# Experts' loop with early row buffers and paired outputs; last batch routed in halves among the shared blocks

## The chip, the cores and the metric

One of the eight cores of a Trainium2 chip runs the kernel. The metric is device time in microseconds (us). Engines: PE (matrix products), ACT, DVE and POOL (elementwise work), SP, which here only starts DMA transfers; POOL starts its own indirect transfers.

## The reference

Four sequences of 1024 tokens, 256 numbers a token. First a power attention with 8 heads, then a layer of 64 experts, each with a residual and a layer norm (bias and constants left out):

```python
a = where(causal, (q @ k.T * scale)**2 * exp(gate), 0)     # 8 heads, 2 query heads a key head
x = layernorm(x + ((a @ v) / (sum(a) + 1e-6)) @ Wc)
scores = softmax(x @ gate_w.T)                              # 64 experts
w, idx = top_k(scores, 6); w /= sum(w)
buf[e, pos] = x[token]                                      # at most 768 rows an expert
eo = silu(buf @ w_gate.T) * (buf @ w_up.T) @ w_down.T       # hidden width 176
y[token] += eo[e, pos] * w                                  # scatter-add
x = layernorm(x + y + shared_swiglu(x))                     # hidden width 352
```

## The kernel before

`schedule()` writes one list of tasks; every engine's program walks that list in order and issues its own part of each task, with semaphores between the engines. So the place of a task in the list sets its place in the queue of each engine that takes part in it. Every fp32 product runs as three passes over a high and a low part (`wf_hi`, `wf_lo`, `xe_hi`, `xe_lo`, ...).

**Attention.** 32 heads (4 batches of 8), each in 20 units (`UNITS`): a unit is 128 keys against a group of 256 queries. PE makes the scores (line 686) and the products with v (1035, 1038); ACT squares; POOL adds the squares up (`nacc`, 1903) and masks the decays (1893, 1894). When a group's units are done, PE's `norm` (1048) sums `nacc` over the keys and projects. The routing of batches 0 to 2 (the steps of `ROUTE`) runs in the background of the next batch's units. Its last steps, `send0` to `send3` on DVE (1683 to 1689), make the slot numbers `slot_u`, and POOL scatters each row to its six experts' lists: `slots<-rows,slot_u`, 48 indirect DMAs of 128 rows a batch (1944).

**Shared blocks.** After attention come 8 blocks of 512 tokens. A block is two half-blocks of `gate_up` (18 products, 686) and `hidden` (ACT and DVE), then `shared_down` (40 products, 696). DVE adds the normed rows `xr`, loaded from `x_dram`, and SP stores the sum to `y_part[0]`. The last batch's routing stands in this list as well, its steps between the blocks (`route_some`); PE makes its `x1t`, `logit` and `count` products (1080, 1095). No expert's rows can be loaded before all scatters have landed (`s_scatter` in `rows_in`).

**Experts.** For each of 64 experts SP loads up to 512 of its rows into one of five buffers `xr` (889), PE transposes them (`turn_x`, 1138) into one of the two spare PSUM banks, ACT and DVE split them into `xe_hi` and `xe_lo`, PE does `gate_up` (18 products of 512 columns, line 686) and `down` (four tiles of 128 rows, 5 products each, 696). ACT scales each tile into one of three buffers `y_e` (1359), and POOL adds it to the tokens' rows in `y_part[x % 2]` by an indirect DMA with addition (1954), whose row numbers it reads from a column of `xr`. `xr` of expert x is free for expert x+5 when the adds of x have landed (`rows_wait`, `c_add`). A list's unused rows point to dummy rows behind the tokens' and are added too. Rows beyond 512 go through 4 jobs at the end: DVE finds them (`jobs`, 1745 to 1757) at expert 2; POOL fetches their rows at experts 32 to 35 (1963).

**End.** `y_part[0] + y_part[1]` is loaded, normed and stored.

Of the kernel before, what the change touches and what calls it, by code (L numbers as in the profile page):

```python
# [63 lines left out]
WS, XS, YS, HS, XE, RS = 4, 5, 3, 4, 4, 4  # L64
# [14 lines left out]
for g_ in range(1, NG):  # L79
# [3 lines left out]
UNITS_ALL = [(n, g, s) for n in range(HEADS) for g, s in UNITS]  # L83


NA, NS, NJ = 7, 2, 4


ROUTE = ([f"stat{j}" for j in range(TILES // 2)] + ["std"] + [f"norm{j}" for j in range(TILES // 2)] + ["store"]
         + [f"{what}{k}" for k in range(NG) for what in ("x1t", "logit")] + ["softmax0", "softmax1", "max", "index"]  # L90
         + [f"{what}{q}" for q in range(4) for what in ("hot", "chosen")] + ["chosen_bf", "weight0", "weight1", "count", "slots"]
         + [f"{what}{q}" for q in range(4) for what in ("again", "send")])

SENDS = 24
# [18 lines left out]
def schedule():  # L113
# [20 lines left out]

    def qkv_tasks(n):
        def column(which, r, tc):
            put_off.append((on_spare("col", n, which, r, tc), ("col_lo", n, which, r, tc)))
# [12 lines left out]
        return tasks  # L150
# [6 lines left out]
    def route_step(b, name):  # L157
        if name[:3] in ("x1t", "log") or name == "count":
            on_spare("route", b, name)
            if name == "count":  # L160
                on_spare("route", b, "taken")
        else:
            do("route", b, name)
            if name[:4] == "send":
                q = int(name[4:])
                to_send.extend(("scatter", b, k) for k in range(q * SENDS // 4, (q + 1) * SENDS // 4))
# [13 lines left out]
    load_at = {4: 3, 11: NG, 13: NG + 1, 18: NG + 2}  # L180

# [48 lines left out]
    for u, (n, g, s) in enumerate(UNITS_ALL):  # L230
        at = u % NU
        catch_up()
        if at == 0:
            if n + 1 < HEADS:
                if (n + 1) % H == 0:
                    must += gate_tasks((n + 1) // H)
                must += qkv_tasks(n + 1)
                first = 2 if (n + 1) % H == 0 else 0
                must_at = [first + i * (NU - ahead - first) // len(must) for i in range(len(must))]
        if u + ahead < len(UNITS_ALL):  # L240
            if UNITS_ALL[u + ahead][0] != n:
# [4 lines left out]
        for what, when in (("em", em_at), ("decay_f", f_at), ("em_mask", mask_at)):  # L246
            if at in when:
                n1, g1 = n + when[at] // NG, when[at] % NG
                if n1 < HEADS and (n1, g1) != (0, 1):
                    do(what, n1, g1)  # L250
        if s == 2 * g - 1:
            do("decay", n, g)
        if s == 2 * g + 1:
            do("yt", n, g)
            late += [(u + 2, "norm", n, g, 0), (u + 2, "project", n, g, 0), (u + 3, "project", n, g, 1)]
        if at in load_at:
            n1, g1 = n + load_at[at] // NG, load_at[at] % NG
            if n1 < HEADS:
                do("decay_in", n1, g1)
        run_late(u)  # L260
        if must and at in must_at:
            must.pop(0)()
        elif background and u >= step_from:
            route_step(n // H - 1, background.pop(0))
            step_from = u + 2
# [28 lines left out]
        if to_send and at in send_at:  # L294
            do(*to_send.pop(0))
        if at == 5 and n % H == 0 and n:
            assert not background and not to_send
            background = list(ROUTE)
# [18 lines left out]
    assert not background  # L317


    background = list(ROUTE)  # L320

    def route_some(count):
        for _ in range(min(count, len(background))):
            route_step(B - 1, background.pop(0))
# [16 lines left out]
    def shared_up(m):  # L341
        for half in range(2):
            do("gate_up", 2 * m + half)
# [19 lines left out]
    route_some(len(background))  # L363
# [3 lines left out]
    def turn(x_id):  # L367
        do("pick", x_id)
        for pair in range(tiles_of(x_id) // 2):
            on_spare("turn_x", x_id, pair)  # L370

    def down(x_id):
        for j in range(tiles_of(x_id)):
            on_spare("down", x_id, j)

    for x_id in range(2):
        do("rows_in", x_id)
    do("raw_in", 2)
    turn(0)
    for x_id in range(E + KJ):  # L380
# [7 lines left out]
        if x_id + 3 < E + KJ:  # L388
            do("raw_in" if x_id + 3 < E else "over_raw", x_id + 3)
        if x_id + 1 < E + KJ:  # L390
            turn(x_id + 1)
        do("gate_up", k)
        do("hidden", k, 0)
# [9 lines left out]
    down(E + KJ - 1)  # L403
# [18 lines left out]
def build(nc, xT, x, wall, wvall, wg, gw, bc, wffn, table, out):  # L422
# [3 lines left out]
    y_part = [nc.dram_tensor(f"y_part{i}", [N + CAP, C], F32).ap() for i in range(2)]  # L426
    x1_dram = nc.dram_tensor("x1_dram", [N, C], F32).ap()
# [21 lines left out]
    masked_nth, nadd_of, unit_of = {}, {}, {}  # L449
    nadd = 0  # L450
    for u, (n, g, s) in enumerate(UNITS_ALL):
        unit_of[n, g, s] = u
        if s >= 2 * g:
            masked_nth[u] = len(masked_nth) + 1
        if s < 2 * g:
# [10 lines left out]
    down_of = {x_id: spare["down", x_id, tiles_of(x_id) - 1] for x_id in range(E + KJ)}  # L466
# [3 lines left out]

    def f_nth(n, g):
        return n * (NG - 1) + g

    def em_nth(n, k):
        return n * NG + k + 1

    with ExitStack() as ctx:
# [48 lines left out]
        row_w = [sb(ctx, f"row_w{i}", [P, MT]) for i in range(XS + KJ)]  # L526
# [8 lines left out]
        with ExitStack() as att:  # L535
# [37 lines left out]
            nacc = [sb(att, f"nacc{i}", [P, R, GROUP]) for i in range(NJ)]  # L573
# [29 lines left out]
        with ExitStack() as last:  # L603
# [30 lines left out]
        s_std, s_sqrt, s_x1, s_x1_out, s_x1t_hi, s_x1t_out = (signal(k) for k in (  # L634
            "s_std", "s_sqrt", "s_x1", "s_x1_out", "s_x1t_hi", "s_x1t_out"))
        s_shift, s_soft, s_token, s_weight = signal("s_shift"), signal("s_soft"), signal("s_token"), signal("s_weight")
        s_chosen, s_slot, s_scatter = signal("s_chosen"), signal("s_slot"), signal("s_scatter")
# [40 lines left out]
        def av_bank(j):  # L678
            return bank[2 + j % NJ]
# [32 lines left out]

        def row_w_of(x_id):
            return row_w[x_id % XS if x_id < E else XS + x_id - E]
# [8 lines left out]
        def rows_wait(once, x_id):  # L723

            prev = x_id - XS
            if prev >= 0:
                once.wait_ge(c_add[prev % 2], added(prev))
            else:
                last = max(m for m in range(M) if m % XS == x_id % XS)
                once.wait_ge(*out_of(("shared_down", last, 1)))  # L730
# [30 lines left out]
        def sp_program(e):  # L761
# [83 lines left out]
            def route(b, name):  # L845
                if name == "store":
                    once.wait_ge(s_x1, b + 1)
                    e.dma_start(x1_dram[b * T:(b + 1) * T, :].rearrange("(j p) c -> p j c", p=P),
                                rows[:, :, 0:C]).then_inc(s_x1_out, 16)
                elif name[:3] == "x1t":  # L850
                    k = int(name[3:])
                    ts = slice(b * T + k * GROUP, b * T + (k + 1) * GROUP)
                    once.wait_ge(s_x1t_hi, b * NG + k + 1)
                    e.dma_start(x1t_dram[0, :, :, ts], f32(x1t_hi[:, :, :])).then_inc(s_x1t_out, 16)
                    once.wait_ge(*out_of(("route", b, name)))
# [8 lines left out]
            def shared_in(m):  # L864
                i, r = m % XE, m % XS
                ms = slice(m * MAIN, (m + 1) * MAIN)
                b = m * MAIN // T
                attention_over(once)
                once.wait_ge(s_x1_out, 16 * (b + 1))
                once.wait_ge(s_x1t_out, 16 * 2 * NG * (b + 1))  # L870
# [4 lines left out]
                if m >= XS:  # L875
# [1302 lines left out]
```

## Time and profile before

| | us |
|---|---|
| median of 3 runs | 2573.97 (2572.37 to 2574.27) |
| profiled execution | 2557.7 |
| its span, first to last instruction | 2555.9 |
| attention, to the last projection | 1757.4 |
| shared blocks and routing, to the first expert's `gate_up` | 1757.4 to 1932.0 |
| experts 0 to 60 | 1932.0 to 2454.4 |
| experts 61 to 63, the jobs, the last adds | 2454.4 to 2513 |
| sums, norm and stores | 2513 to 2555.9 |
| busy: PE / DVE / ACT / POOL | 2312 / 1398 / 1249 / 1578 |

The stages follow one another, so each has to be read by itself. A wait is charged to the engine and line that waited, and `<-` names what ended it.

### The profile page before, as it was taken

How to read it: one execution, taken by the hardware profiler on the slowest of the kernel's cores; microseconds unless marked ns; L12 is line 12 of the kernel's file. 1: busy time of each engine (PE TensorE's matmuls, PEld its weight loads, DVE VectorE, ACT ScalarE, POOL GpSimd, SP SyncE). 2: the span in 40 equal slices, each digit the busy share in tenths (PEclk: the TensorE clock that was granted, in tenths of full speed). 3: DMA queues.
4: the chain of work that ended last, by engine and by line, in shares of the span. 5: the costliest groups of instructions: out<-in, count | busy, mean ns of one | idle time of the engine just before them, and what ended most of it. 6: DMA issues, size and time to landing. Idle time of an engine off the chain costs nothing.

```text
span 2555.9 us, 34620 instructions
## 1 busy us (share of the span) xinstructions
PE 2312.3 (90%) x11876; PEld 1793.6 (70%) x11880; DVE 1397.8 (55%) x2813; ACT 1248.9 (49%) x2302; POOL 1578.3 (62%) x1421
## 2 busy tenths in 40 slices
PE   5999999999999899999999999998797999989981
PEld 4777776776767677776667777666685887778871
DVE  2444444445564454557445455745666766656664
ACT  3444444444434344343444443434234777767764
POOL 2566555544578654457855445784074888788885
PEclk8999999999999999999999999999798999999996
DMA  3766741122123112111411211224355999889987
GB/s 125 302 238 261 279 157 63 54 63 64 40 64 119 54 52 87 40 40 69 138 31 53 88 40 38 71 76 146 119 188 163 216 212 202 193 197 213 210 165 230
DMA packets 162663, 329.68 MB, mean 129 GB/s; under 512 B 17552, under 2 KB 98192, under 8 KB 162480
## 3 DMA queue, kind: packets, MB, share of 16 engines
q1 hardware_dynamic: 114144, 262.01, 30.4%
q0 software_dynamic: 48192, 65.04, 14.0%
q8 instruction: 97, 1.59, 0.3%
q14 instruction: 86, 0.70, 0.1%
q10 hardware_dynamic: 144, 0.33, 0.0%
HBM read 172.21 MB, written 155.11 MB: 128 GB/s over the span
## 4 chain that ended last, share of the span: by engine, by line
PE 61%; POOL 10%; DMA 9%; DVE 8%; issue 7%; ACT 5%; POOLq 0%; SPq 0%; ACTq 0%; DVEq 0%
PE bank L686 37%; PE bank L1038 13%; POOL slots L1944 4%; DMA y_part<-y_e,xr 4%; PE bank L696 4%; POOL nacc L1903 3%; PE bank L1048 3%; DMA xr<-slots 3%; POOL y_part L1954 2%; PE bank L1138 2%; PE bank L1035 1%; DVE acc L1563 1%; DMA w_raw_f<-in_wffn,job_w 1%; ACT a L1288 1%; DVE ub L1526 1%
## 5 line engine op out<-in xcount | busy, mean ns | idle before, releaser
L1903 POOL TENSOR_TENSOR nacc<-nacc,a 128x512 f32<-128x512 f32 (+1 forms) x384 | 448.0, 1167 | 286.7 <-ACT a L1292 137.6
L1038 PE MATMUL bank<-a,v 128*128 128x512 f32 x1024 | 529.3, 598 | 0.0
L1954 POOL DMA_INDIRECT y_part<-y_e,xr x256 | 436.5, 1705 | 119.2 <-issue 74.5
L1288 ACT ACTIVATE a<-bank,c_s 128x512 f32<-128x512 f32 x384 | 263.7, 687 | 164.2 <-PE bank L686 148.5
L686 PE MATMUL bank<-q_hi,k_hi 128*128 128x512 f32 (+1 forms) x640 | 324.4, 507 | 12.1 <-DVE ub L1526 6.0
L1292 ACT ACTIVATE a<-ub 128x512 f32<-128x512 f32 (+1 forms) x256 | 133.9, 523 | 394.5 <-DVE ub L1526 382.9
L1903 POOL TENSOR_TENSOR nacc<-a,a 128x512 f32<-128x512 f32 (+1 forms) x128 | 148.9, 1163 | 252.1 <-ACT a L1288 194.6
L1944 POOL DMA_INDIRECT slots<-rows,slot_u x192 | 198.3, 1033 | 163.0 <-DVE slot_u L1689 110.9
L1563 DVE SCALAR_TENSOR_TENSOR acc<-bank,rec,acc 128x256 f32<-128x256 f32 x512 | 223.3, 477 | 98.5 <-PE bank L686 94.5
L686 PE MATMUL bank<-q_lo,k_hi 128*128 128x512 f32 (+1 forms) x640 | 240.0, 375 | 0.0
L686 PE MATMUL bank<-q_hi,k_lo 128*128 128x512 f32 (+1 forms) x640 | 238.3, 372 | 0.0
L686 PE MATMUL bank<-xt_hi,w_hi 128*128 128x512 f32 x384 | 189.8, 494 | 34.8 <-DVE acc L1563 31.0
L686 PE MATMUL bank<-xe_hi,wf_hi 128*128 128x512 f32 (+3 forms) x504 | 206.2, 409 | 10.2 <-DMA xe_lo<-x1t_dram 10.2
L686 PE MATMUL bank<-wc_hi,yt_hi 128*128 128x256 f32 x512 | 205.7, 402 | 4.9 <-DVE acc L1563 4.9
L1038 PEld LDWEIGHTS bank<-a,v 128*128 128x128 f32 x1024 | 186.3, 191 | 33.2
L686 PE MATMUL bank<-xe_lo,wf_hi 128*128 128x512 f32 (+3 forms) x504 | 198.6, 394 | 0.0
L686 PE MATMUL bank<-xe_hi,wf_lo 128*128 128x512 f32 (+3 forms) x504 | 198.1, 393 | 0.0
L1504 DVE TENSOR_TENSOR q_lo<-bank,q_hi 128x512 fp32r<-128x512 f32 x128 | 88.5, 691 | 184.7 <-ACT q_hi L1267 184.7
L1048 PEld LDWEIGHTS bank<-ones,nacc 128*128 128x128 f32 x1024 | 133.5, 193 | 75.2 <-issue 60.8
L1267 ACT ACTIVATE q_hi<-bank 128x512 fp32r<-128x512 f32 x128 | 76.2, 596 | 214.8 <-PE bank L686 214.6
L1542 DVE TENSOR_TENSOR yt_lo<-bank,yt_hi 128x512 fp32r<-128x512 f32 x128 | 88.5, 691 | 168.9 <-ACT yt_hi L1300 168.9
L686 PEld LDWEIGHTS bank<-q_hi,k_hi 128*128 128x128 f32 x640 | 122.6, 192 | 71.5 <-issue 35.9
(212 smaller groups left out, 5671.6 us busy)
## 6 DMA issues: line engine op xcount, KB each, us to landing
slots<-acc SPq DMA_DIRECT2D x65, 816.0 KB, 7.2
w_raw_f<-in_wffn SPq DMA_DIRECT2D x66, 624.0 KB, 6.7
xr<-slots SPq DMA_DIRECT2D x64, 544.0 KB, 4.6
decay_all<-decay_dram SPq DMA_DIRECT2D x128, 128.0 KB, 3.4
w_hi<-w_dram SPq DMA_DIRECT2D x24, 384.0 KB, 4.7
w_lo<-w_dram SPq DMA_DIRECT2D x24, 384.0 KB, 5.4
sum<-y_part SPq DMA_DIRECT2D x16, 512.0 KB, 10.7
wc_hi<-wc_dram SPq DMA_DIRECT2D x24, 256.0 KB, 3.9
```

The lines of the kernel that those rows point to most:

```text
L686: ins = e.matmul(dst, a, b, start=first and i == 0, stop=last and i == len(passes) - 1, skip_group_check=True)
L696: ins = e.matmul(dst, a, b, start=first and n_ == 0 and p_ == 0, stop=n_ == len(steps) - 1 and p_ == len(passes) - 1, skip_group_check=True)
L1038: e.matmul(dst, v[n % 3][:, s, :], a32[u % NA][:, :, :], start=first, stop=False, skip_group_check=True).then_inc(s_av)
L1048: ins = e.matmul(av_bank(j)[:, k:k + 1], nacc[j % NJ][:, r, tt * P:(tt + 1) * P], ones[:, 0:1], start=(k == 0), stop=True, skip_group_chec ...
L1288: e.activation(squares, score_bank(u)[:, 0:R * w].rearrange("p (r t) -> p r t", r=R), ACT.Square, scale=c_s[b % 2][:, g * (g - 1) + s, h:h ...
L1292: e.activation(squares, ub[masked_nth[u] % 2][:, :, 0:w], ACT.Square).then_inc(s_sq)
L1504: e.tensor_tensor(lo, bank[6 + m % 2][:, :], f32(hi), ALU.subtract).then_inc(s_out_of[m % 2])
L1542: e.tensor_tensor(yt_lo[j % 2][:, :, :], av_bank(j)[:, :].rearrange("p (r t) -> p r t", r=R), f32(yt_hi[j % 2][:, :, :]), ALU.subtract).th ...
L1563: ins = e.scalar_tensor_tensor(out=part, in0=bank[6 + m % 2][:, tt * C:(tt + 1) * C], scalar=rec[j % 2][:, tt * R + r:tt * R + r + 1], in1 ...
L1903: e.tensor_tensor(out_, a, b, op).then_inc(s_nadd)
L1944: e.indirect_dma_start(out=slots, out_offset=bass.IndirectOffsetOnAxis(ap=slot_u[:, j, k:k + 1], axis=0), in_=rows[:, j, :], in_offset=Non ...
L1954: e.indirect_dma_start(out=y_part[part], out_offset=bass.IndirectOffsetOnAxis(ap=x_rows[:, j, TOKEN_COL:TOKEN_COL + 1].bitcast(U32), axis= ...
```

## The change

The experts' loop, with the buffers it touches (XS counts `xr`, YS counts `y_e`):

```diff
-WS, XS, YS, HS, XE, RS = 4, 5, 3, 4, 4, 4
+WS, XS, YS, HS, XE, RS = 4, 4, 4, 4, 4, 4
+KEPT = 8
 # rows_wait: when the buffer of expert x_id is free
-                once.wait_ge(c_add[prev % 2], added(prev))
+                once.wait_ge(s_spare, spare["turn_x", prev, MT // 2 - 1] + 1)
+                once.wait_ge(c_pick, prev + 1)
 # pick, DVE: keeps the row numbers
+                elif x_id >= KEPT:
+                    once.wait_ge(c_add[x_id % 2], added(x_id - KEPT))
+                e.tensor_copy(row_token[kept_at(x_id)][:, 0:n], rows_of(x_id)[:, 0:n, TOKEN_COL].bitcast(U32))
 # add_rows, POOL: unused rows now point to row NOWHERE
-                    in_=y_e[y][:, j, :], in_offset=None, bounds_check=N + CAP - 1, oob_is_err=True,
+                    in_=y_e[y][:, j, :], in_offset=None, bounds_check=N - 1, oob_is_err=False,
 # down: one task, and one spare bank, for two tiles; ACT still evicts and POOL still adds tile by tile
-        for j in range(tiles_of(x_id)):
-            on_spare("down", x_id, j)
+        for pair in pairs:
+            if pair < tiles_of(x_id) // 2:
+                on_spare("down", x_id, pair)
 # schedule, one expert
-        if x_id + 1 < E + KJ:
-            turn(x_id + 1)
-        do("gate_up", k)
+        do("gate_up", k, 0)
         do("hidden", k, 0)
+        if x_id + 1 < E + KJ:
+            turn(x_id + 1)
         ...
+        do("gate_up", k, 1)
         do("hidden", k, 1)
         ...
+        do("gate_up", k, 2)
         do("hidden", k, 2)
         if x_id:
-            down(x_id - 1)
+            down(x_id - 1, (0,))
         do("hidden", k, 3)
+        if x_id:
+            down(x_id - 1, (1,))
```

So the spare banks are used four times an expert instead of six, and an expert's rows are turned between the first and the second third of the gate products of the expert before it.

The last batch's routing is cut into two halves of 512 tokens, parts 3 and 4, of 27 steps each. Part 3's steps go one to a unit among the last 21 units of attention; its last six, and all 24 of its scatters, stand behind `gate_up` of half-block 0. Part 4's steps stand between `gate_up` and `hidden` of half-blocks 1 to 11:

```diff
+PARTS = [(b_, 0, TILES) for b_ in range(B - 1)] + [(B - 1, t_, TILES // 2) for t_ in (0, TILES // 2)]
-    route_some(10)
+    paces = [len(background) - 27, 4, 2, 1, 2, 2, 2, 3, 3, 2, 4, 2]
     shared_up(0)
     for m in range(M):
         ...
-        route_some(7)
         for pair in range(MAIN // GROUP):
             on_spare("shared_down", m, pair)
+        if m == M - 1:
+            do("rows_in", 0)
+            do("rows_in", 1)
         do("shared_out", m)
-        route_some(6)
 # in the loop over attention's units
-        if to_send and at in send_at:
+        if to_send and (at in send_at or n >= LAST):
             do(*to_send.pop(0))
+        if u - u_last == first_half_routed_at:
+            background = route_steps(B - 1)
```

The units of the last two heads are interleaved (`LAST_UNITS`), so that all groups of the last batch's first half are finished early; the tables `last_at` and `cols_at` place their decays and columns. Batch 2's last scatters, formerly one pair to about every second unit, go one pair to a unit from head 30 on.

`shared_down` is evicted by a copy on ACT instead of the addition on DVE: the normed rows are stored straight into `y_part[1]`, which formerly was filled with zeros, and the 8 loads of normed rows go.

```diff
-                e.tensor_tensor(y_e[y][:, js, :], bank[6 + m % 2][:, :].rearrange("p (j c) -> p j c", c=C), xr[r][:, js, 0:C],
-                                ALU.add).then_inc(s_out_of[m % 2])
+                e.activation(y_e[y][:, js, :], bank[6 + m % 2][:, :].rearrange("p (j c) -> p j c", c=C), ACT.Copy).then_inc(s_out_of[m % 2])
```

On SP, around the first experts, before (`xr<-slots` are an expert's rows, `w_raw_f` its weights, `y_part<-y_e` a block's store; `c_add` counts landed adds):

```order
L882 DMA y_part<-y_e 128x4x256 [waits s_out_of1,s_out_of0] x4
L889 DMA xr<-slots 128x1088 [waits s_scatter]
L889 DMA xr<-slots 128x1088
L862 DMA w_raw_f<-in_wffn 128x1248 [waits c_wl]
L889 DMA xr<-slots 128x1088
L862 DMA w_raw_f<-in_wffn 128x1248 [waits c_wl]
L889 DMA xr<-slots 128x1088
L862 DMA w_raw_f<-in_wffn 128x1248 [waits c_wl]
L889 DMA xr<-slots 128x1088
L862 DMA w_raw_f<-in_wffn 128x1248 [waits c_wl]
L889 DMA xr<-slots 128x1088 [waits c_add0]
```

and after:

```order
L961 DMA y_part<-y_e 128x4x256 [waits s_out_of1,s_out_of0] x3
L968 DMA xr<-slots 128x1088 [waits s_scatter]
L968 DMA xr<-slots 128x1088
L961 DMA y_part<-y_e 128x4x256 [waits s_out_of1,s_out_of0]
L946 DMA w_raw_f<-in_wffn 128x1248 [waits c_wl]
L968 DMA xr<-slots 128x1088
L946 DMA w_raw_f<-in_wffn 128x1248 [waits c_wl]
L968 DMA xr<-slots 128x1088
L946 DMA w_raw_f<-in_wffn 128x1248 [waits c_wl]
L968 DMA xr<-slots 128x1088 [waits c_pick,s_spare]
```

The first two loads of rows have moved ahead of the last block's store, and from the fifth on a load waits for the turn (`s_spare`) and the pick of the expert four before it in place of the adds.

On POOL, in head 30 (`slots<-rows` are batch 2's scatters, `nacc` the sums of squares), before:

```order
L1944 DMA slots<-rows,slot_u 49920x272 x2
L1903 TENSOR_TENSOR nacc<-a_5,a_6 128x512
L1903 TENSOR_TENSOR nacc<-nacc,f_b 128x512
L1918 COPY nacc<-a_0 128x2x128
L1944 DMA slots<-rows,slot_u 49920x272 x2
L1903 TENSOR_TENSOR nacc<-a_0,a_1 128x2x128
L1944 DMA slots<-rows,slot_u 49920x272 x2
L1903 TENSOR_TENSOR nacc<-a_2,a_3 128x512
L1893 TENSOR_TENSOR decay_all<-decay_all,tab 128x128
L1894 TENSOR_TENSOR decay_all<-decay_all,tab 128x128
L1903 TENSOR_TENSOR nacc<-nacc,a_4 128x512
```

and after:

```order
L2029 DMA slots<-rows,slot_u 49920x272 x2
L1990 TENSOR_TENSOR nacc<-a_5,a_6 128x512
L1990 TENSOR_TENSOR nacc<-nacc,f_b 128x512
L2029 DMA slots<-rows,slot_u 49920x272 x2
L2004 COPY nacc<-a_0 128x2x128
L2029 DMA slots<-rows,slot_u 49920x272 x2
L1990 TENSOR_TENSOR nacc<-a_0,a_1 128x2x128
L2029 DMA slots<-rows,slot_u 49920x272 x2
L1990 TENSOR_TENSOR nacc<-nacc,a_2 128x512
L2029 DMA slots<-rows,slot_u 49920x272 x2
L1990 TENSOR_TENSOR nacc<-nacc,a_3 128x2x128
L2029 DMA slots<-rows,slot_u 49920x272 x2
```

A pair of scatters now stands behind every unit's work, where two or three adds stood between pairs.

## Rows read from the trace of the kernel before

**Rows 1.** The page's part 4, by engine: shares of the chain that ended last

```profile
PE 61%; POOL 10%; DMA 9%; DVE 8%; issue 7%; ACT 5%; POOLq 0%; SPq 0%; ACTq 0%; DVEq 0%
```

**Rows 2.** Windows: busy us (count) of PE, PEld, DVE, ACT, POOL; clock; DMA; GB/s

```profile
1757.40:1767.90 10.50, 0.28 (x4) 0.08 (x2) 5.07 (x9) 3.77 (x3) 2.02 (x5) 0.67 0.76 262
1767.90:1932.00 164.10, 126.65 (x703) 109.55 (x705) 100.65 (x203) 47.65 (x78) 52.94 (x48) 0.85 0.51 176
1932.00:2454.40 522.40, 487.93 (x2788) 408.93 (x2787) 354.15 (x558) 387.49 (x668) 415.85 (x245) 0.98 0.89 201
2454.40:2513.00 58.60, 41.94 (x273) 37.14 (x271) 29.76 (x54) 32.04 (x66) 49.07 (x32) 0.93 0.72 117
2513.00:2556.00 43.00, 0.00 (x0) 0.00 (x0) 20.99 (x88) 19.30 (x41) 18.86 (x9) 0.50 0.77 298
```

**Rows 3.** Groups by shape, POOL, 1660:1757.4: busy us, mean ns | idle before

```profile
L1944 POOL DMA_INDIRECT slots<-rows,slot_u x30 | 29.6, 987 | 7.3 <-issue 5.6 <-POOL nacc L1903 1.6
L1903 POOL TENSOR_TENSOR nacc<-nacc,a 128x512 f32<-128x512 f32 x20 | 25.7, 1283 | 1.6
```

**Rows 4.** Timeline, attention's end: start, length [idle before <- releaser]

```profile
1664.96 0.99 POOL L1944 DMA_INDIRECT slots<-rows,slot_u  x1 [0.15 <-POOL nacc L1903]
1707.62 0.59 PE L1035 MATMUL bank<-a,v 128*128 128x256 f32 x2
1714.96 1.84 PE L1048 MATMUL bank<-ones,nacc 128*128 128x1 f32 x8 [4.07 <-POOL nacc L1903]
```

**Rows 5.** Waits, 1767 to 1932 us: us in total, times, longest

```profile
POOL slots L1944 <- DVE slot_u L1689: 94.5, 1, 94.5
POOL slots L1944 <- issue: 14.3, 47, 0.3
PE bank L1095 <- DVE chosen_bf L1644: 14.0, 1, 14.0
PE bank L1138 <- DMA xr<-slots: 13.7, 1, 13.7
```

**Rows 6.** Chain of waits, 1840 to 1960 us: start, us, what

```profile
1924.24 3.52 DMA xr<-slots
1927.81 1.13 PE bank L1138 x4
```

**Rows 7.** Chain of waits, experts, 2050 to 2120 us

```profile
2055.97 6.83 DMA y_part<-y_e,xr
2062.82 5.54 DMA xr<-slots
2069.50 4.15 PE bank L686 x18
2073.65 2.62 PE bank L696 x20
2076.33 1.16 PE bank L1138 x8
```

**Rows 8.** Waits, experts, 1932 to 2454.4 us

```profile
PE bank L1138 <- DMA xr<-slots: 25.2, 27, 4.2
PE bank L696 <- DVE xe_lo L1778: 6.2, 1, 6.2
```

**Rows 9.** Groups by line, POOL, 1932 to 2454.4 us

```profile
L1954 POOL DMA_INDIRECT y_part<-y_e,xr x237 | 404.4, 1706 | 113.4 <-issue 68.7 <-ACT y_e L1359 41.6 <-DMA y_part<-y_e,xr 3.0
L1963 POOL DMA_INDIRECT acc<-slots,job_rows x8 | 11.6, 1454 | 2.4 <-issue 2.1 <-DMA y_part<-y_e,xr 0.3
```

**Rows 10.** Timeline, POOL and DVE, 2263 to 2290 us

```profile
2268.30 1.55 POOL L1954 DMA_INDIRECT y_part<-y_e,xr  x1 [0.30 <-issue]
2268.77 1.45 DVE L1694 TENSOR_TENSOR wf_lo<-w_raw_f,wf_hi 128x1248 fp32r<-128x1248 f32 x1
2277.61 2.04 POOL L1954 DMA_INDIRECT y_part<-y_e,xr  x1 [0.30 <-issue]
2278.87 0.68 DVE L1708 TENSOR_TENSOR ha_lo<-h_a,ha_hi 128x512 fp32r<-128x512 f32 x1
```

More of the change, by code:

```diff
@@ L82, with before, diagonal, route_steps @@
 NU = len(UNITS)
[L83 to L94, printed above, removed]
+def before(n, g):
+    return [(n, g, s) for s in range(2 * g)]
+def diagonal(n, g):
+    return [(n, g, 2 * g), (n, g, 2 * g + 1)]
+LAST = HEADS - 2
+LAST_UNITS = (before(LAST, 1) + diagonal(LAST, 0) + diagonal(LAST, 1) + diagonal(LAST + 1, 0) + before(LAST + 1, 1)
+              + before(LAST, 2) + diagonal(LAST + 1, 1) + before(LAST, 3) + diagonal(LAST, 2) + diagonal(LAST, 3)
+              + before(LAST + 1, 2) + before(LAST + 1, 3) + diagonal(LAST + 1, 2) + diagonal(LAST + 1, 3))
+UNITS_ALL = [(n, g, s) for n in range(LAST) for g, s in UNITS] + LAST_UNITS
+GROUPS = [(n, g) for n, g, s in UNITS_ALL if s == 2 * g + 1]
+GROUP_NTH = {group: i for i, group in enumerate(GROUPS)}
+NA, NS = 7, 2
+PARTS = [(b_, 0, TILES) for b_ in range(B - 1)] + [(B - 1, t_, TILES // 2) for t_ in (0, TILES // 2)]
+def route_steps(p):
+    pairs = range(PARTS[p][2] // 2)
+    steps = ([f"stat{j}" for j in pairs] + ["std"] + [f"norm{j}" for j in pairs] + ["store"]
+             + [f"{what}{k}" for k in pairs for what in ("x1t", "logit")] + ["softmax0", "softmax1", "max", "index"]
+             + [f"{what}{q}" for q in pairs for what in ("hot", "chosen")] + ["chosen_bf", "weight0", "weight1", "count", "slots"]
+             + [f"{what}{q}" for q in pairs for what in ("again", "send")])
+    return [(p, step) for step in steps]
+SENDS = 6
 def f32(ap):
@@ L229, in schedule @@
         do("score", u)
-    for u, (n, g, s) in enumerate(UNITS_ALL):
-        at = u % NU
+    for u, (n_, g, s) in enumerate(UNITS_ALL):
+        n, at = divmod(u, NU)
         catch_up()
[L233 to L239, printed above, removed]
+        if at == 0 and n < LAST:
+            if (n + 1) % H == 0:
+                must += gate_tasks((n + 1) // H)
+            must += qkv_tasks(n + 1)
+            first = 2 if (n + 1) % H == 0 else 0
+            must_at = [first + i * (NU - ahead - first) // len(must) for i in range(len(must))]
         if u + ahead < len(UNITS_ALL):
-            if UNITS_ALL[u + ahead][0] != n:
+            if (u + ahead) // NU != n:
                 while must:
@@ L342, in shared_up @@
         for half in range(2):
-            do("gate_up", 2 * m + half)
+            for i in range(3):
+                do("gate_up", 2 * m + half, i)
+            route_some(paces[2 * m + half])
             hidden(2 * m + half)
-    route_some(10)
+    paces = [len(background) - 27, 4, 2, 1, 2, 2, 2, 3, 3, 2, 4, 2]
+    assert sum(paces) == len(background)
+    paces += [0] * (2 * M - len(paces))
     shared_up(0)
@@ L362, in schedule, with down @@
             do("split_lo", m - 2)
-    route_some(len(background))
+    assert not background and not to_send
     do("counted",)
     def turn(x_id):
-        do("pick", x_id)
         for pair in range(tiles_of(x_id) // 2):
             on_spare("turn_x", x_id, pair)
-    def down(x_id):
-        for j in range(tiles_of(x_id)):
-            on_spare("down", x_id, j)
-    for x_id in range(2):
-        do("rows_in", x_id)
+        do("pick", x_id)
+    def down(x_id, pairs):
+        for pair in pairs:
+            if pair < tiles_of(x_id) // 2:
+                on_spare("down", x_id, pair)
     do("raw_in", 2)
@@ L465, in build @@
             raw_loads += 1
-    down_of = {x_id: spare["down", x_id, tiles_of(x_id) - 1] for x_id in range(E + KJ)}
+    down_of = {x_id: spare["down", x_id, tiles_of(x_id) // 2 - 1] for x_id in range(E + KJ)}
     shared_down_of = {m: spare["shared_down", m, 1] for m in range(M)}
@@ L886, in rows_in @@
                 r = x_id % XS
[L887 removed]
+                all_sent(once)
                 rows_wait(once, x_id)
@@ new lines, in route @@
+                    once.wait_ge(s_chosen, p + 1)
+                    e.matmul(head, strict_bf[:, :], chosen_bf[:, tiles_in(p), :], start=True, stop=False, skip_group_check=True)
+                    for j in range(nt - 1):
+                        ins = e.matmul(head[:, j + 1:nt, :], ones_bf[:, :],
+                                       chosen_bf[:, t0 + j:t0 + j + 1, :].to_broadcast([P, nt - 1 - j, E]), start=False,
+                                       stop=(j == nt - 2), skip_group_check=True)
+                else:
+                    for j in range(nt):
+                        ins = e.matmul(ps[:, 0:E], ones_bf[:, :], chosen_bf[:, t0 + j, :], start=(j == 0), stop=(j == nt - 1))
@@ L1110, in gate_up @@
-            def gate_up(k):
+                product(e, bank[3 * (k % 2) + part][0:cols.stop - cols.start, 0:width], [
+                    (g_hi[:, c, cols], g_lo[:, c, cols], x_hi[:, c, :], x_lo[:, c, :]) for c in range(CC)]).then_inc(c_gu)
+            def gate_up(k, part):
                 w, i = job_of(k)
@@ L1171, in over_body @@
                 e.wait_ge(c_h, 2 * (k - 1))
-                gate_up_passes(k, w, xe_hi[0][:, :, 0:OVER], xe_lo[0][:, :, 0:OVER], OVER)
+                for part in range(3):
+                    gate_up_part(k, part, w, xe_hi[0][:, :, 0:OVER], xe_lo[0][:, :, 0:OVER], OVER)
                 e.wait_ge(c_hl, 2 * k + 2)
@@ L1581, in route @@
                     steps_done()
-                    for j in range(TILES):
+                    for j in each:
                         ins = e.bn_aggr(mv[:, j, :], stats[:, j, :])
@@ L1630, in route @@
                     steps_done()
-                    for j in range(TILES):
+                    for j in each:
                         ins = e.max_index(out=top8_at[:, j, :], in_max=top8[:, j, :], in_values=scores[:, j, :])
```

452 lines of the change are left out of this document (238 added, 214 removed).

## The prediction

> **What bounds the kernel now.** I read the page's chain first, then the windows by stage, then the waits and the chain inside each stage. The chain [rows 1] is PE for 61%, with POOL and DMA for about a tenth each; an average, so the windows [rows 2] come next. There the reader should see four different limits. In the shared blocks and routing (1767.9 to 1932.0) PE works 126.65 of 164.1 us. Its long waits are two [rows 5]: 14.0 us for `chosen_bf`, and 13.7 us for the first expert's rows, at the end of a chain: DVE makes `slot_u`, POOL scatters 48 times, the last scatter lands at 1924.24, the load takes 3.52 us, PE turns at 1927.81 [rows 6]. In the experts (1932.0 to 2454.4) PE works 487.93 of 522.4 us. The chain there [rows 7] is either PE's own period, 4.15 + 2.62 + 1.16 = 7.93, with gaps about 7.98, or a detour: landing of adds 6.83 us, then the load of rows 5.54 us, which waited for them, then PE. PE lost 25.2 us to such loads and 6.2 us once behind `jobs` on DVE [rows 8]. From 2454.4 to 2513 POOL's adds set the end, 49.07 us busy of 58.6. The last 43 us, which the change leaves alone, stay as they are.
>
> **Experts' loop.** The wait on adds leaves SP's queue; on that queue stand the weight loads, which were held up behind it. Rows of x+4 now wait for the turn and pick of x, four periods earlier than they are needed, against a load of 5.54 us [rows 7]. So the 25.2 us go. What is late next? The candidates are POOL and the two spare banks. POOL: 237 adds, mean 1.706 us [rows 9], start to start 0.30 more, as between two scatters, 14.3 us in 47 gaps [rows 5]: 2.006, four an expert 8.02. This is PE's 7.98 to within the reading. At their best the adds take 1.55 [rows 10], 7.4 an expert, so POOL can catch up half a us a period. Skipping unused rows is not in the trace; of four adds of 1.56 it saves between nothing and, at a quarter of the rows unused, 1.56 us. I take nothing, since no row shows that an add's length follows its rows. DMA moves less by it: its share of 0.89 [rows 2] need not rise with the pace.
>
> Eight fetches for the jobs at experts 32 to 35 cost POOL 8 × (1.454 + 0.30) = 14 us [rows 9]. Before, this lag passed through `c_add` to PE at once. Now four `y_e` buffers let POOL lag about two periods, 16 us, so PE does not feel it; the lag melts at up to half a us a period over 28 experts, 14 us, and the rest (0 to 12, I take 3) is paid after expert 61. The paired banks leave four uses an expert, each about 1.16 to 1.3 of PE, then ACT, then DVE for a turn: my sum round them is 7.0 to 7.2 us, an estimate just below the period. ACT's 387 and DVE's 354 of 522 us [rows 2] leave room for the small copy of row numbers, so it costs nothing; without that cover, some 0.2 us a period, 12 in all. So experts 0 to 61: 60 × 7.98 + 5.4 (the first, without `down`: 7.98 − 2.62) + 6.2 (`jobs`, bounds 0 to 8.7) = 490.4 against 522.4: −32.0. With the lag of 3: **−29** (range −10 to −36).
>
> A rule speaks against this. Two adds of 1.55 and 2.04 lie in [rows 10]: the first beside DVE's `wf_lo`, the second beside `ha_lo`, both with two inputs in SBUF. The Trainium skill, "GPSIMD Engine Reference", its opening table, says that POOL shares its SBUF interfaces with VectorE and contends with DVE instructions that have two SBUF inputs. By that rule all of `wf_lo`, `ha_lo` and `hb` would be added to a nearly always busy POOL. The trace agrees for `ha_lo` at most, and not for `wf_lo`: 1.55 beside it. The mean of 1.706 holds what is so stretched now.
>
> **Shared blocks.** Before: 10.5 + 164.1 = 174.6 us from the end of attention to expert 0. After, POOL has 24 scatters behind the last `send` instead of 48. A scatter costs 52.94/48 + 0.30 = 1.40 [rows 2, 5], so 33.6 us. The sends stand behind half-blocks 10 and 11, so PE has then done eleven half-blocks of gate products, 11 × 4.15, four blocks of downs, 4 × 2 × 2.62, at a granted clock below full at first, 4 us more, and 4 us of routing products: 74.6. DVE, which has the routing of a half-block in front of `hidden`, comes 12 to 15 us later: 88.5. Then 33.6, landing 1.5, load 3.5, turn and split 4.2 (1927.81 to 1932.0): 131.3. PE's own sum is shorter: 8 × (2 × 4.15 + 2 × 2.62) = 108, with the same 8 and some waits 116 to 123. The first half's 24 scatters are hidden, as POOL had nothing there (its wait was 94.5 us long [rows 5]). DVE's eviction goes to ACT, busy 47.65 of 164.1 [rows 2]. The loads of normed rows and the zero fills lie on queues with room, at nothing. So 10.5 + 131.3 = 141.8, **−32.8** (range −40, PE alone, to −25, DVE 8 us later).
>
> **Attention's end.** Here the change costs. POOL's rows are nearly gapless there, 30 scatters at 0.987 us and adds of 512 at 1.283 [rows 3]. PE already waited 4.07 us for `nacc` at 1714.96 [rows 4]. In the new order a pair of scatters (0.99 + 0.30 + 0.98 and some idle, 2.35) stands behind every unit of head 30. From POOL's place at 1664.96 [rows 4] to the mask of head 31, group 1, stand 14 pairs, 32.9 us, and about 21 us of adds and masks: POOL is there at 1718.5. PE's norm for that group comes just behind the av that ran at 1707.62 [rows 4], and waits. What is left for PE behind that norm: 42.7 us from 1714.96 to 1757.7 as before, 3.3 that formerly ran ahead of its wait, 1.4 net for half the routing's short products against one group's norm and projections that are done sooner (an estimate, 0 to 5): 47.4. End 1765.9 instead of 1757.4: **+8.5** (range 0, POOL shorter, to +20, a second such wait).
>
> **Sum.** −29 − 32.8 + 8.5 = −53.3; I round the shared stage's and attention's unknown waits up by 2: −51. The profiled execution took 2557.7 us, span 2555.9 and 1.8 around it; it would become 2506.7. The median of the runs, 2574.0, stands 16.3 above that execution, and I move it by the same amount: 2523.
>
> **Rivals.**
> 1. POOL paces the loop. For: 8.02 against 7.98, and the fetches. Against: at 1.55 it would be faster than PE. Time: POOL's 277 instructions of both windows take 415.85 + 49.07 us [rows 2] and 277 × 0.30 between them, 548, against 568 from expert 0's first add, 13 us behind 1932 (4.15, `hidden` and 2.62), to 2513: −20; 6 to 7 of that is lost again behind `jobs`: −13 instead of −29. With the others 2537.
> 2. The chain round the two spare banks is longer than the period. A turn for x+1 now lies inside `gate_up` of x, so `xe_hi`, `xe_lo`, `pick`, `h_a`, `split_lo`, `hb` and `y_e` follow on ACT and DVE in one row, and a down can't start before the turn's bank is evicted. For: ACT and DVE are 74% and 68% busy, in strict order. Against: my sum of 7.0 to 7.2. The other stages give −24, so from a period of 8.86 the change is slower than before (522.4 + 24 = 546.4, less 11.6 and the lag of 3, over 60). At 9.2 it is 2574 + 20 = 2594.
> 3. Attention's end is later by 23 instead of 8.5, if PE stands a second time behind POOL, masks and scatters in a row: 2537. For: POOL's rows; against: after the 14 pairs only adds are left.
> 4. By the rule of two SBUF inputs, each period of POOL is 7.4 + 1.45 + 0.68 + 0.69 = 10.2 instead of 7.98, 64 times: some 2665. The adds of 1.55 beside `wf_lo` speak against it.
>
> **How the numbers follow.** Forecast 0.62; rival 1: 0.20; rival 3: 0.11; rival 2: 0.05; rival 4: 0.02. The forecast's own terms reach from −76 to −15, the ends seldom all together, so 2500 to 2545 holds most of it; rivals 1 and 3 lie inside. Range 2498 to 2552. The measurement tells 0.2%, about 5 us, from no change: faster 0.92, same 0.03, slower 0.05 (rivals 2 and 4, less the mild ends of 2, and a little for what I did not see).
>
> **What would show it.** Attention's last product near 1766, with PE waiting some 8 us for `nacc` before the norm of head 31, group 1. PE's first turn about 127 us after the first `gate_up`, and the last scatter just before it; 24 scatters between the blocks. In the experts no wait of PE for `xr`, periods of 7.98 except around `jobs`, the same through experts 32 to 40; POOL's wait for `y_e` small. It is wrong if PE waits for ACT or DVE in most periods, if periods stay near 8.5, or if the first turn still stands behind `xr` by more than 10 us.

## The result

The changed kernel takes 2553.99 us (median of 5 runs, 2550.01 to 2560.44) against 2573.97 (2566.74 to 2578.99): ratio 0.993 (0.9915 to 0.9944), some 20 us less where 51 were forecast, and just outside the range given. Side by side on another occasion the two took 2540.46 and 2557.58, ratio 0.9931 (0.9907 to 0.9955). The runs below were made on three chips, and the kernel before differs from one to the next: 2557.6 us on chip 3, 2573.4 on chip 13, 2554.9 on chip 9 (for the first result the chip is not on record). So each run is set against the kernel before on its own chip.

The windows of the changed kernel, by the same stages as [rows 2] (busy us and count of PE, PEld, DVE, ACT, POOL; granted clock; DMA share; GB/s):

```profile
1771.60:1781.40 9.80, 0.00 (x0) 0.00 (x0) 4.08 (x6) 3.77 (x3) 1.92 (x4) 0.67 0.75 266
1781.40:1926.40 145.00, 122.08 (x664) 102.52 (x664) 79.52 (x160) 54.86 (x92) 52.35 (x49) 0.93 0.45 151
1926.40:2440.00 513.60, 479.90 (x2861) 412.92 (x2862) 358.78 (x641) 364.13 (x681) 416.21 (x240) 0.98 0.83 192
2440.00:2507.00 67.00, 32.93 (x206) 29.73 (x204) 21.10 (x43) 23.08 (x51) 55.92 (x37) 0.76 0.50 79
2507.00:2549.00 42.00, 0.00 (x0) 0.00 (x0) 19.86 (x88) 19.30 (x41) 19.64 (x10) 0.50 0.78 303
```

Attention ends at 1771.6 (1757.4 before). The shared blocks and routing take 145 us (164.1 before). The loop and its tail take as long as they did: 513.6 + 67.0 against 522.4 + 58.6.

The chain of the changed kernel by engine, against [rows 1]:

```profile
PE 53%; POOL 16%; issue 12%; DVE 9%; ACT 5%; DMA 4%; POOLq 0%; another core or an unknown queue 0%; SPq 0%; ACTq 0%; DVEq 0%
```

DMA's share has fallen from 9% to 4%, as it should when no load of rows waits for adds, and POOL's has risen from 10% to 16%. POOL's groups in the loop, against [rows 9], show why:

```profile
L2039 POOL DMA_INDIRECT y_part<-y_e,row_token x232 | 407.0, 1754 | 109.9 <-issue 67.7 <-ACT y_e L1450 38.9 <-DMA y_part<-y_e,row_token 3.3
L2047 POOL DMA_INDIRECT acc<-slots,job_rows x8 | 9.6, 1205 | 2.4 <-issue 2.4
```

The add has not become shorter but longer: 1.754 us in place of 1.706. And PE, which no longer waits for `xr`, waits for ACT's `y_e`, which waits for adds to land before it may overwrite an output buffer (1926 to 2440 us):

```profile
ACT y_e L1450 <- DMA y_part<-y_e,row_token: 52.8, 20, 5.7
PE bank L1216 <- ACT y_e L1450: 27.2, 24, 3.9
```

[rows 8] had 25.2 us of PE on rows. The wait changed its name and kept its size, because behind both stood POOL's adds. POOL had hardly been idle before, either. From the first add to the last, its 264 adds took 448.9 us, the 0.30 us in front of each instruction 81.3 and the fetches 11.6, which leaves 25.8 of 567.6; in the changed kernel 458.4, 81.3 and 9.6 leave 18.2 of 567.6. Waits taken off PE could shorten the loop by no more than this idle time, as long as the adds did not get shorter.

**Where an add gets long.** The timeline of POOL and DVE in two periods of the changed kernel, some 120 us into the loop:

```profile
2041.78 1.54 POOL L2039 DMA_INDIRECT y_part<-y_e,row_token  x1 [0.30 <-issue]
2042.03 1.45 DVE L1785 TENSOR_TENSOR wf_lo<-w_raw_f,wf_hi 128x1248 fp32r<-128x1248 f32 x1
2043.51 0.69 DVE L1797 TENSOR_TENSOR h_b<-bank,silu_b 48x512 f32<-48x512 f32 x1
2043.63 2.60 POOL L2039 DMA_INDIRECT y_part<-y_e,row_token  x1 [0.30 <-issue]
2044.12 0.68 DVE L1799 TENSOR_TENSOR ha_lo<-h_a,ha_hi 128x512 fp32r<-128x512 f32 x1
...
2049.49 1.45 DVE L1785 TENSOR_TENSOR wf_lo<-w_raw_f,wf_hi 128x1248 fp32r<-128x1248 f32 x1
2050.24 2.11 POOL L2039 DMA_INDIRECT y_part<-y_e,row_token  x1 [0.30 <-issue]
2052.38 0.69 DVE L1802 TENSOR_TENSOR hb<-h_b,hb 48x512 fp32r<-48x512 f32 x1
2052.66 1.83 POOL L2039 DMA_INDIRECT y_part<-y_e,row_token  x1 [0.30 <-issue]
```

What counts is what DVE does at the moment an add *starts*. At 2041.78 no such operation runs yet; `wf_lo` begins 0.25 later, lies beside the rest of the add, and the add takes its 1.54. At 2050.24 `wf_lo` is running and ends 0.70 later: the add takes 0.57 longer. At 2052.66 `hb` ends 0.41 later: 0.28 longer. At 2043.63 `h_b` runs with `ha_lo` right behind it; `ha_lo` ends 1.17 after the add's start: 1.05 longer. The add loses the time to the end of the operation, less some 0.12 (of `ha_lo`'s end where that follows at once). Counted over 256 adds of each trace (the first eight left out), by DVE's operation at the start; "lost" is the sum of the lengths over 1.55:

| DVE at the add's start | SBUF operands | before: adds, lost us | after: adds, lost us |
|---|---|---|---|
| `wf_lo` | two | 53, 33.1 | 36, 19.1 |
| `hb` | two | 55, 4.2 | 28, 7.1 |
| `ha_lo` | two | 7, 0.4 | 3, 0.1 |
| `h_b`, `ha_lo` behind it | one, then two | 0 | 23, 22.9 |
| `h_a` | one | 10, 0.1 | 26, 0.0 |
| `xe_lo` | one | 16, 0.1 | 56, 0.0 |
| nothing or a short one | | 115, 0.8 | 84, 0.0 |

Back to back, POOL's period is 4 × 1.85 and what it loses, and its starts walk through PE's period of 7.43 until they meet every one of these operations. PE's own period, which the prediction had left at 7.98, had fallen to 7.43, and it bought nothing.

### The profile page after: what moved, and what is told of

Its sections match the earlier page's. It is cut to its first block, busy times and chain, and to the rows that moved or that the text cites. A ratio compares the mean times of both kernels' runs of the same rounds, so it can differ in the third digit from the quotient of the medians.

```text
span 2549.3 us, 34748 instructions
## 1 busy us (share of the span) xinstructions
PE 2296.0 (90%) x11880; PEld 1786.2 (70%) x11880; DVE 1383.8 (54%) x2884; ACT 1227.5 (48%) x2323; POOL 1585.3 (62%) x1422
## 4 chain that ended last, share of the span: by engine, by line
PE 53%; POOL 16%; issue 12%; DVE 9%; ACT 5%; DMA 4%; POOLq 0%; another core or an unknown queue 0%; SPq 0%; ACTq 0%; DVEq 0%
PE bank L769 33%; PE bank L1117 12%; POOL y_part L2039 8%; POOL nacc L1990 4%; PE bank L1127 3%; POOL slots L2029 3%; DMA y_part<-y_e,row_token 2%; PE bank L779 2%; PE bank L1114 1%; DVE acc L1653 1%; ACT a L1370 1%; DVE ub L1618 1%; DVE yt_lo L1632 1%; ACT yt_hi L1381 1%; ACT a L1374 0%
## 5 line engine op out<-in xcount | busy, mean ns | idle before, releaser
L2039 POOL DMA_INDIRECT y_part<-y_e,row_token x264 | 458.4, 1736 | 119.8 <-issue 77.5
L2029 POOL DMA_INDIRECT slots<-rows,slot_u x192 | 197.6, 1029 | 138.3 <-DVE slot_u L1780 86.7
```

The source lines that it names most:

```text
L2029: e.indirect_dma_start(out=slots, out_offset=bass.IndirectOffsetOnAxis(ap=slot_u[:, j, k:k + 1], axis=0), in_=rows[:, j, :], in_offset=Non ...
L2039: e.indirect_dma_start(out=y_part[part], out_offset=bass.IndirectOffsetOnAxis(ap=token, axis=0), in_=y_e[y][:, j, :], in_offset=None, boun ...
```

## The experiments

The changed kernel's second execution and the three runs behind it are from chip 3, the two with the routing moved, the dummy rows and the undivided `gate_up` from chip 13, the last four from chip 9.

**The changed kernel again**, as a partner for the next three.

> The changed kernel once more, as the partner for the next runs. Both theories: 2554, within 6; POOL again adds back to back from expert 3 to the end, with a mean near 1.74 us an add.

2540.46 (0.9931), mean add 1.736; less than the 2554 expected, as the kernel before is faster on this chip too. This execution is the better one to hold against [rows 2], as its routing stage lacks the stalls that the first has (last section): attention to 1773.5, then 142.9 us to expert 0, loop from first to last add 565.4 us, against 1757.7, 174.3 and 567.6 before.

**`h_a` and `h_b` in PSUM.** The product is written back into its own bank, so `ha_lo` and `hb` have one operand in SBUF; PE's wait before it overwrites the bank moves from `c_h` to `c_hl`.

```diff
-e.tensor_tensor(h_a[:, 0:width], bank[b0 + 1][:, 0:width], silu_a[:, 0:width], ALU.mult).then_inc(c_h)
+e.tensor_tensor(bank[b0 + 1][:, 0:width], bank[b0 + 1][:, 0:width], silu_a[:, 0:width], ALU.mult).then_inc(c_h)
-e.tensor_tensor(ha_lo[i][:, 0:width], h_a[:, 0:width], f32(ha_hi[i][:, 0:width]), ALU.subtract).then_inc(c_hl)
+e.tensor_tensor(ha_lo[i][:, 0:width], bank[b0 + 1][:, 0:width], f32(ha_hi[i][:, 0:width]), ALU.subtract).then_inc(c_hl)
 # h_b, hb, ACT's reads of h_a and h_b likewise
-                once.wait_ge(c_h, 2 * (k - 1))
+                once.wait_ge(c_hl, 2 * (k - 1))
```

> h_a and h_b are written back into their PSUM banks instead of SBUF, so the DVE operations ha_lo and hb read one operand from SBUF instead of two; nothing else changes. Theory 1 (an add of POOL that starts while a DVE operation with two SBUF operands runs, or is about to run, waits until that operation ends; in the trace after, the adds that start in wf_lo lose 19 us, in hb 7 us, in h_b with ha_lo behind it 23 us, all others nothing): the 30 us of hb and ha_lo go, the starts shift and wf_lo takes some 5 more; mean add 1.64, time 2554 - 25 = 2529 (2522 to 2539). Theory 2 (the long adds wait for room in the DMA queue): mean add and time unchanged within 5 us. Theory 3 (PE's period, 7.43, sets the loop and POOL only follows): unchanged.

2504.98, ratio 0.9795 (0.9772 to 0.9819); 35.5 us less than the changed kernel on the same chip, and 2502.18, 0.98, on chip 9. POOL's adds over the whole run, from the changed kernel's again and from this one:

```profile
L2039 POOL DMA_INDIRECT y_part<-y_e,row_token x264 | 458.4, 1736 | 111.1 <-issue 73.1
```

```profile
L2037 POOL DMA_INDIRECT y_part<-y_e,row_token x264 | 415.9, 1575 | 117.6 <-issue 80.9
```

DVE's work is the same, some operations even 0.01 to 0.02 us longer; 42.5 us of POOL's time are gone. `ha_lo`, `hb` and `h_b` now cost the adds 0.1 us in all, and `wf_lo` 5.6 instead of 19. My reading, which no run tested by itself: a POOL that runs at PE's pace keeps its place in the period and meets `wf_lo` less. I had expected the opposite there, hence 35 us instead of 25. Theories 2 and 3 fall.

**And `wf_lo` shortened** to 16 columns from expert 4 on; the low parts of the other weights are left out.

```diff
+                cols = slice(0, 16) if 4 <= x_id < E else slice(None)
-                e.tensor_tensor(wf_lo[w][:, :], w_raw_f[r % RS][:, :], f32(wf_hi[w][:, :]), ALU.subtract).then_inc(c_wl)
+                e.tensor_tensor(wf_lo[w][:, cols], w_raw_f[r % RS][:, cols], f32(wf_hi[w][:, cols]), ALU.subtract).then_inc(c_wl)
```

> As the run before, and from expert 4 on wf_lo is computed for 16 of its 1248 columns only (the low parts of the other weights are those of an earlier expert, so the output is not the reference's). Theory 1: no add is longer than 1.6 but for the four of expert 60 and later, 7.4 us of POOL an expert against 7.43 of PE; time 2554 - 45 = 2509 (2503 to 2517). Theory 2: as the changed kernel, 2554.

2497.08 (0.9769, 0.9743 to 0.9796): mean add 1.556, lost 1.6 us in all, the floor. 8 us less than the run before; in the traces 5.4 of it is the loop (519.3 us), and 4.4 is an attention that ended earlier, which the edit does not touch. The estimate of 45 in sum was 43.

**The kernel before with `h_a` and `h_b` in PSUM.**

> The kernel before with h_a and h_b in PSUM. Theory 1: there 33 of the 39 us that its adds lose are lost in wf_lo and only 5 in hb and ha_lo, so 2574 - 3 (2564 to 2576). Theory 2: unchanged. If it gains 20 us or more, the gain of the second run is not from the adds.

2547.66 (0.9968, 0.9953 to 0.9983), 10 us less, where 3 were expected: the adds take 3.3 us less in all (mean 1.69), as expected, and the rest is not explained here. `wf_lo` still costs 34.5 us. With it the table is closed; us from the first add to the last:

| | `h_a`, `h_b` in SBUF | in PSUM |
|---|---|---|
| loop before | 567.6 | 560.2 |
| loop changed | 565.4 | 524.7 |

The change of the loop is worth 2 us with `h_a` and `h_b` in SBUF and 35.5 with them in PSUM; executions of one kernel differ by 1 to 2 us here. Of the 35.5, 29.7 are shorter adds (445.6 us in all against 415.9), since `wf_lo` costs 34.5 us in one kernel and 5.6 in the other. The kernel before without `wf_lo`'s share was not run, so what the change is worth with no contention at all is not shown.

**The last batch's first half routed after attention**, and then also the scatters at their old places.

```diff
         if u - u_last == first_half_routed_at:
             assert not background
-            background = route_steps(B - 1)
-    background += route_steps(B)
+    background = route_steps(B - 1) + route_steps(B)
 # the second of the two, besides
-        if to_send and (at in send_at or n >= LAST):
+        if to_send and at in send_at:
```

> The changed kernel with all 27 steps of part 3's routing behind gate_up of half-block 0; the units' order and the scatters of batch 2 as in the changed kernel. Of the 14 to 16 us by which attention ends later, theory 1 puts about 5 on DVE, whose routing steps stand in front of acc, nrm and ub in the last 21 units, and 6 on PE's wait for nacc behind POOL's scatters. Then attention ends near +10 instead of +15, and the shared stage grows by 10 to 15 us (21 steps of DVE in front of hidden 0): +5 to +10 against the changed kernel. Rival: the interleaved heads alone cost it; then attention's end stays at +15, and the whole is +12 or more.

> As the run before, and batch 2's scatters at every second unit, as in the kernel before; what is left of them goes behind gate_up of half-block 0. Theory 1: the wait of 5.6 us for nacc in head 30 goes, attention ends at +4 or less against before. Rival: attention's end unchanged against the run before, so POOL's scatters were not its cause.

2565.03 (0.9964) and 2563.10 (0.9958). The changed kernel's 0.9931 is from chip 3, and on chip 13, where these ran, it was not measured, so these ratios do not say that they are slower. What can be set beside them are the next two runs, from the same chip and with the routing as changed (`h_a` and `h_b` in PSUM): attention ends there at 1773.4 and 1773.7 and expert 0 starts at 1949.1 and 1950.3. Here attention ends at 1763.6 and 1760.4 and expert 0 starts at 1941.1 and 1933.9, 8 us earlier and more.

So the routing steps cost attention 10 us. They lie behind the norm of head 31, group 1: from its start to attention's end it is 53.4 to 54.0 us in all nine executions with the steps in attention, and 44.8 without them. They are not DVE's alone, at which I had put 5: from 1555 us to attention's end PE is busy 5.0 us less than in the run with dummy rows (192.6 against 197.6; the steps' 32 products are 3.7 of it) and idle 4.8 less. In the second run the wait for `nacc` did not go, as expected, but moved to the next group's norm and grew. PE's waits in attention's last 100 us there:

```profile
PE bank L1126 <- POOL nacc L1989: 8.0, 1, 8.0
PE bank L1116 <- DVE nrm L1637: 0.6, 1, 0.6
```

Its 3 us are no more than two executions of one kernel differ by (1757.7 and 1760.0 before), so what POOL's scatters cost attention and what the units' order costs it is not told apart.

Behind attention the steps save little on this chip: the way to expert 0 is 177.5 and 173.4 us, against 175.7 and 176.7 with the routing as changed. On the other two chips, where that way takes 143 to 147 us, this was not tried.

**Unused rows added to dummy rows again** (with PSUM): `base=N`, `bounds_check=N + CAP - 1`, `y_part` of `N + CAP` rows.

> The changed kernel with h_a and h_b in PSUM, and unused rows added to dummy rows again instead of skipped. Theory: an add's length on POOL does not follow the rows that it moves (1.55 us undisturbed in both kernels), so the time is that of the same kernel with skipping, 0.9795 of before, within 4 us; DMA's share in the loop rises by some 0.05. Rival: DMA, at 0.89 before, is next in line and sets the pace: 10 us or more longer.

2534.11 (0.9851, 0.9823 to 0.9879), 13 us over the expected time by the ratio of the kernel with skipping; but not in the loop, which takes 522.9 us (524.7 with skipping) at a mean add of 1.579. The longer part is the routing stage, 176 us instead of 145, with the stalls of the last section; all four runs from this chip have them. DMA's share from 1940 to 2450 is 0.96 instead of 0.83, and nothing waits for it. Skipping saves transfers, not time.

**The turn in front of an undivided `gate_up`** (with PSUM; the pairs stay).

```diff
-        do("gate_up", k, 0)
-        do("hidden", k, 0)
         if x_id + 1 < E + KJ:
             turn(x_id + 1)
+        for i in range(3):
+            do("gate_up", k, i)
+        do("hidden", k, 0)
         ...
-        do("gate_up", k, 1)
         ...
-        do("gate_up", k, 2)
```

> The changed kernel with h_a and h_b in PSUM, and the turn of the next expert in front of an undivided gate_up, as before. Theory: with POOL at 7.4 to 7.6 us an expert, PE is now next to it (7.43); its period goes back to 7.95 and the loop to about 61 x 7.95, so 20 to 28 us longer than with the divided gate_up. Rival: POOL still sets the pace alone, and the place of the turn is worth less than 6 us.

2578.63 (1.0016, 1.0002 to 1.0031): slower than the kernel before. Some of it is the routing stage (177 us), but the loop takes 572.3 instead of 524.7, twice what I expected. The chain of one period:

```profile
2055.51 4.15 PE bank L766 x18
2059.66 1.21 PE bank L776 x10
2060.87 0.02 issue
2060.90 0.84 ACT y_e L1447 x2
2061.74 0.03 issue
2061.76 0.60 ACT hb L1421
2062.36 0.03 issue
2062.39 0.85 ACT y_e L1447 x2
2063.23 0.04 issue
2063.28 0.66 PE bank L1213 x4
```

This is the prediction's rival 2: the turn waits for a spare bank, the bank for ACT's two evictions, and these stand behind `hb`. 8.43 us a period, more than the 7.98 before. So pairs with the turn where it was make the loop slower than the 560.2 of the kernel before with `h_a` and `h_b` in PSUM; in the changed kernel the first third of `gate_up`, 6 products and 1.4 us, stands between the downs and the turn, and in its periods of 7.43 PE does not wait.

**The old buffers** (with PSUM): `XS, YS = 5, 3`, and `rows_wait` on `c_add`.

> The changed kernel with h_a and h_b in PSUM, but five row buffers that are free only when the adds of the expert have landed, and three output buffers, as before; pairs and divided gate_up stay. Theory: POOL's 14 us of fetches pass to PE through the rows again, and each late landing too; 10 to 25 us longer than with early free rows. Rival: with undisturbed adds POOL is never late enough, and the buffers are worth less than 5 us.

2513.92 (0.985, 0.9829 to 0.987), 12 us over its partner (2502.18); in the traces 8 of it is the loop (531.8 against 523.7). The old wait is back:

```profile
PE bank L1213 <- DMA xr<-slots: 20.8, 18, 3.1
```

Of the 35.5 us that the loop's change is worth with `h_a` and `h_b` in PSUM, the early free rows and the fourth output buffer are thus some 8 to 12.

The partner's expectation:

> The second run's kernel again, as the partner of the two others: 0.9795 of before, within 0.003.

**The kernel before, once more.**

> The kernel before once more, one look. Theory: an execution near its median has the same loop, 560 to 570 us from the first add to the last, adds of 1.70 us, and what separates 2574 from 2558 lies in the routing stage, where PE stands at issue. Rival: the loop itself is 15 us longer, with longer adds.

2558.79, span 2557.0: much as the first (mean 1.705, loop 566.6, attention's end to expert 0 174.4), and PE does not stand at issue in the routing stage. It is from chip 9, where the kernel before takes 2554.9, so it does not say what the 2573 on chip 13 consist of.

**Jobs early**: with PSUM, `jobs` and its eight fetches before expert 0.

```diff
-        if x_id == 2:
-            do("jobs")
-        if E // 2 <= x_id < E // 2 + KJ:
-            do("over_rows", E + x_id - E // 2)
     do("raw_in", 2)
+    do("jobs")
+    for q in range(KJ):
+        do("over_rows", E + q)
     turn(0)
```

> The changed kernel with h_a and h_b in PSUM, and the jobs found and their rows fetched before expert 0 instead of at expert 2 and at experts 32 to 35. If POOL is what ends the loop, its 14 us of fetches now fall where it still waits for the first outputs (34 us in the second run), and the stall of 6 us behind jobs goes, while expert 0 starts 2 to 4 us later: 8 to 15 us less than the same kernel without it. If PE ends it, 0 to 4 us.

2485.54 (0.9728, 0.9715 to 0.9742): 17 us less than its partner, a little more than the 8 to 15 expected, and 69 less than the kernel before; the best version. The loop from first to last add is 503.2 us, 20 less; expert 0 starts 3 us later.

## Why the prediction was wrong

By its steps, with the changed kernel's second execution (its span is 17 us shorter than that of the trace before):

- **Attention's end**, forecast +8.5: +15.8. The mechanism held: PE waited for `nacc` before the norm of head 31, group 1, which started at 1719.7 (1718.2 in the first execution; 1718.5 forecast); the wait was 4.6 us and not 8, as PE came later too. The step that failed is the 1.4 us net for half the routing's products, which left 47.4 us behind that norm. It was 53.9, and 44.8 without the routing steps.
- **Shared blocks**, forecast −32.8, 141.8 us to expert 0: 142.9 us, −31.4. Right in size and in path. POOL's 24 scatters took 33.6 us from 1874.8, the last one led to the load and the load to the turn, and PE waited 1.2 us for those rows, so its own chain was hardly shorter:

```profile
1907.39 2.54 DMA slots<-rows,slot_u
1909.94 3.79 DMA xr<-slots
1913.77 0.67 PE bank L1216 x4
```

  In the first execution it was 154.9 us and only −19.5, with the stalls of the last section, and there PE's own chain ended last.
- **Experts' loop**, forecast −29: −2 (0 in the first execution). This is the step that made the forecast wrong: "At their best the adds take 1.55 [rows 10], 7.4 an expert, so POOL can catch up half a us a period". It set POOL's 8.02 beside PE's 7.98 as equal "to within the reading" and took the better end. POOL was late at every expert from the third on and never caught up for long: the adds' mean was 1.736, and POOL's idle time in the loop fell from 25.8 to 16.5 us, so there was little to gain. The first sentence of the loop's part was right: the 25.2 us of waits for rows went. That the loop gave 35.5 us with `h_a` and `h_b` in PSUM, near the forecast, is luck. The forecast's 29 were mainly the 25.2 us of waits for rows, at a period of 7.98 that stayed; early rows and the fourth output buffer measured 8 to 12, and the rest goes with a period of 7.43 and with adds that meet `wf_lo` less.
- **Rival 1**, POOL paces the loop, is what happened, at a chance of 0.20; its −13 was too good, since it kept the mean of 1.706, and the new places of the adds made 1.736, 8 us more over 264.
- **Rival 4**, the rule of two SBUF inputs in the Trainium skill, "GPSIMD Engine Reference", Specifications, had the cause, at 0.02. I read 1.55 beside `wf_lo` as evidence against the rule, and 2.04 beside `ha_lo` as its one trace. The first add had started 0.47 us before `wf_lo`. The second had started 1.26 before `ha_lo`, and in a `wf_lo` that [rows 10] leaves out and that ended 0.61 later:

```profile
2276.77 1.45 DVE L1694 TENSOR_TENSOR wf_lo<-w_raw_f,wf_hi 128x1248 fp32r<-128x1248 f32 x1
```

  The trace agrees with the rule: 49.2 us of contention, all of it in adds that start in an operation with two SBUF operands or in `h_b` with such an operation right behind it. My price, each such operation in full (2.82 us a period, 180 in all), was nearly four times too high.
- **Rival 2** did not occur in the change, but its mechanism is real, at 8.43 us, in the run with an undivided `gate_up`. **Rival 3** did not occur: there was no second long wait for `nacc`.

## What to carry to other kernels

When a wait on a slow engine's result is removed, price that engine alone, back to back, at the mean of its instructions and not at their best, and add up its idle time in the stage: no more than that can be gained while its instructions keep their length. Here it was 25.8 of 567.6 us. When an instruction comes in two lengths, sort its occurrences by what the neighbouring engine was doing at the *start*, before calling one of the lengths noise. Here two intermediate results moved from SBUF to PSUM were worth 35 us, more than the whole change. And compare runs from one chip with one another: here the routing stage took 30 us longer on one chip than on two others.

## What was not expected of the hardware

An add of POOL loses the time to the end of a DVE operation with two SBUF operands that runs at its start, less 0.12 us (0.13 in the mean of 56 such adds of the changed kernel), and the one add that started 0.02 us before such an operation lost nothing. DVE loses nothing the other way round: the 57 `wf_lo` that begin while an add runs take their 1.45 us, 1.48 at most. An add also loses time if a one-operand operation runs that a two-operand one follows at once (`h_b`, then `ha_lo`: 22 of 23). Behind `h_a`, which `wf_lo` follows as closely, 26 adds lost nothing. ACT's `wf_hi`, for which `wf_lo` waits, had ended before each of these 26 began, so that is not the reason; it stays open.

On chip 13 PE stands at "issue" during the last scatters, for nothing that the trace shows. PE in the run with dummy rows:

```profile
1915.30 0.28 PE L777 MATMUL bank<-wf_hi,hb 112*128 112x256 f32 x1 [2.41 <-issue]
1916.71 0.37 PE L777 MATMUL bank<-wf_lo,hb 112*128 112x256 f32 x1 [1.14 <-issue]
1917.42 0.37 PE L777 MATMUL bank<-wf_hi,ha_hi 128*128 128x256 f32 x1 [0.34 <-issue]
```

Over that stage it is 18 us there, and 8, 8 and 16 in the three other runs from chip 13; 7 in the first execution of the changed kernel; none in the eight from chips 3 and 9. ACT stands at issue there too, 11 us in the run with dummy rows. With the routing as changed the stage takes 176 and 177 us on chip 13, 155 in the first execution and 143 to 147 on the other chips; its mean granted clock is 0.86 to 0.87 of full speed on chip 13 and 0.93 to 0.94 in the others. So it seems to go with the chip, or with the hour at which that chip ran; no kernel was traced both there and on another chip. The kernel before has no trace from chip 13, either; that its 16 us more there are the same stalls is likely and not shown. The cause stays open.
